# Waits on landed gathers in GpSimd's queue of a four-layer graph network

## The reference

```python
edge_index = jnp.stack([src, dst])
x = x + L0_gnn(layernorm(x), edge_index)   # attention over 4 heads of the rows x[src[:n]] and x[dst[:n]], n = 3125
x = x + L0_ffn(layernorm(x))               # the best 1561 of the nodes go through a 256-1024-256 network
x = x + L1_gnn(layernorm(x), edge_index)   # relu(segment_sum((x @ W)[src] * norm, dst) + b)
x = x + L1_ffn(layernorm(x))               # attention over 64 slices, 8 heads
x = x + L2_gnn(layernorm(x), edge_index)   # as L1_gnn, with other weights
x = x + L2_ffn(layernorm(x))               # mixture of 8 experts, the best two per node
x = x + L3_gnn(layernorm(x), edge_index)   # graph attention, 8 heads: softmax over the edges of a target
x = x + L3_ffn(layernorm(x))               # mixture of 8 experts, two for all nodes
```

## Time and profile before

| what | value |
|---|---|
| median of 3 runs | 2577.74 us |
| lowest and highest run | 2570.55 and 2579.27 us |
| profiled execution, first to last instruction (span) | 2994.7 us |
| its time around the span | not given |
| PE busy | 2247.6 us, 75% |
| VectorE busy | 1684.2 us, 56% |
| GpSimd busy | 1306.1 us, 44% |
| ScalarE busy | 561.2 us, 19% |
| bytes moved by DMA | 252.62 MB, of them 206.43 MB by gathers |

### The profile page before, as it was taken

How to read it: one execution, slowest core, us unless ns; L and a number is a source line. 1 busy time by engine, 2 the same in 40 slices (tenths; PEclk the granted TensorE clock), 3 DMA queues, 4 the chain that set the end, 5 groups by cost and what they waited for, 6 DMA issues and landing times.

```text
span 2994.7 us, 35813 instructions
## 1 busy us (share of the span) xinstructions
PE 2247.6 (75%) x10818; PEld 1674.7 (56%) x10819; DVE 1684.2 (56%) x4704; ACT 561.2 (19%) x1129; POOL 1306.1 (44%) x1347
## 2 busy tenths in 40 slices
PE   1359955576778778915888978897688888887797
PEld 1347743344444444714766767775566666665576
DVE  2585424455546564835566666656567676765343
ACT  1332310011111111301222222232011101110232
POOL 7101135566556530065555565501666666662000
PEclk8669976798888897957898988998677787777899
DMA  6100032333333313164444444401333333331100
GB/s 186 38 4 25 26 93 78 87 101 95 88 94 96 99 55 102 52 196 122 123 123 121 117 128 120 121 7 62 89 88 91 87 89 88 90 87 30 39 12 24
DMA packets 118568, 252.62 MB, mean 84 GB/s; under 512 B 35491, under 2 KB 61469, under 8 KB 118414
## 3 DMA queue, kind: packets, MB, share of 16 engines
q0 software_dynamic: 70816, 206.43, 25.0%
q1 hardware_dynamic: 44382, 44.41, 4.7%
q10 hardware_dynamic: 3216, 0.01, 0.1%
HBM read 229.33 MB, written 21.43 MB: 84 GB/s over the span
## 4 chain that ended last, share of the span: by engine, by line
PE 45%; DVE 19%; another core or an unknown queue 15%; issue 14%; ACT 3%; DVEq 3%; POOL 1%; DMA 0%; ACTq 0%; SPq 0%
PE PB L990 6%; DVE ACC L1729 6%; PE PB L863 4%; PE PB L637 3%; PE PB L588 3%; PE PB L555 3%; PE PB L640 3%; PE PB L543 2%; PE PB L874 2%; PE PB L582 2%; PE PB L954 2%; PE PB L806 2%; PE PB L969 1%; DVE ACC L2215 1%
## 5 line engine op out<-in xcount | busy, mean ns | idle before, releaser
L453 POOL DMA_INDIRECT BIG<-table,SRCI x832 | 825.1, 992 | 707.4 <-DMA table<-ACC 234.5
L1729 DVE TENSOR_TENSOR ACC<-ACC,PB 128x256 f32 x832 | 348.5, 419 | 540.2 <-remote 249.9
L453 POOL DMA_INDIRECT BIG<-parts,SRCI x416 | 399.1, 959 | 467.5 <-DMA parts<-BIG 197.3
L990 PE MATMUL PB<-BIG,WA 128*128 128x264 f32 x832 | 355.1, 528 | 72.5 <-DVE BIG L2119 46.5
L637 PE MATMUL PB<-BIG,OH 128*128 128x256 f32 x832 | 268.3, 452 | 145.5 <-DVE ACC L1729 123.2
L640 PE MATMUL PB<-BIG,OH 128*128 128x256 bf16 x1248 | 190.5, 296 | 131.6 <-DVE ACC L1729 94.7
L637 PEld LDWEIGHTS PB<-BIG,OH 128*128 128x128 f32 x832 | 164.0, 219 | 182.1 <-DVE ACC L1729 116.1
L640 PEld LDWEIGHTS PB<-BIG,OH 128*128 128x128 bf16 x1248 | 125.8, 105 | 191.1 <-issue 112.0
L2215 DVE TENSOR_TENSOR ACC<-ACC,PB 128x264 f32 x416 | 176.9, 425 | 85.0 <-PE PB L990 46.1
L2119 DVE TENSOR_TENSOR BIG<-BIG 128x256 f32<-128x256 f32 x416 | 157.1, 419 | 117.3 <-ACT BIG L1270 112.5
L863 PE MATMUL PB<-XT,WA 128*128 128x256 f32 (+1 forms) x832 | 215.2, 412 | 10.2 <-ACT HT L1232 10.2
(11 more groups left out here) (465 smaller groups left out, 3318.3 us busy)
## 6 DMA issues: line engine op xcount, KB each, us to landing
BIG<-table,SRCI POOLq DMA_INDIRECT x832
BIG<-parts,SRCI POOLq DMA_INDIRECT x416
table<-ACC SPq DMA_DIRECT2D x10, 660.0 KB, 3.4
swtab<-HT SPq DMA_DIRECT2D x25, 256.0 KB
BIG<-swtab SPq DMA_DIRECT2D x25, 256.0 KB, 3.9
parts<-BIG SPq DMA_DIRECT2D x5, 960.0 KB, 4.1
X<-in_x SPq DMA_DIRECT2D x1, 3072.0 KB
out<-X SPq DMA_DIRECT2D x4, 640.0 KB
```

What stands on the lines that cost most here:

```text
L453: g.indirect_dma_start(out=ring[:, k * width:(k + 1) * width], out_offset=None, in_=rows, in_offset=bass.IndirectOffsetOnAxis(ap=SRCI[:, n ...
L990: pe.matmul(PB[k % 4][:, 0:ROW], OH4[:, (q * GRP + k) * P:(q * GRP + k + 1) * P], G[:, (q * GRP + k) * ROW:(q * GRP + k + 1) * ROW], start ...
L1729: v.tensor_tensor(dst, dst, bank[:, k % 2 * D:(k % 2 + 1) * D], ALU.add).then_inc(sem(f"{st}_acc"), 1)
```

## The change

GpSimd gets three more kinds of wait, and nothing else changes: no gather, buffer or size, and no other engine's program. In the head attention it waits, before the ten gathers of a chunk, until the ten of the chunk ahead have landed. Before the first gather of dst it waits for the last chunk, and after each eight of them for the last four ahead. In gather_slots it waits before each group but a stage's first until the eight gathers of the group ahead have landed; that wait stands in front of the one for PE.

```diff
             for t in range(NT):
+                if t and t % CH == 0:
+                    g.wait_ge(sem(f"g0_in{t // CH - 1}"), 16 * 2 * CH)
                 for buf, n in ((FROM_COL, t), (FROM_ROW, NT + t)):
                     g.indirect_dma_start(out=buf[:, t * D:(t + 1) * D], out_offset=None, in_=a["x"],
...
             g.wait_ge(sem("d_given"), 2)
             for t in range(NT):
+                if t % 8 == 0:
+                    if t:
+                        g.wait_ge(sem(f"d_in{(t // 4 - 1) % 4}"), 16 * 4 * ((t // 4 - 1) // 4 + 1))
+                    else:
+                        g.wait_ge(sem(f"g0_in{NC - 1}"), 16 * 2 * CH)
                 if t >= D_RING and t % 4 == 0:
                     g.wait_ge(sem("d_within"), t - D_RING + 4)
...
                 for n in range(SLOTS):
                     q = n // GRP % NG
                     if n % GRP == 0:
+                        if n:
+                            g.wait_ge(sem(f"slot_in{(q - 1) % NG}"), landed_before(st) + 16 * GRP * ((n - GRP) // BODY + 1))
                         g.wait_ge(sem(f"{st}_mm"), n + GRP)
```

## The result

| | before | after |
|---|---|---|
| median of the runs (4 and 4, side by side) | 2574.14 us | 2822.64 us |
| lowest and highest | 2569.98 and 2579.27 | 2817.98 and 2830.22 |
| ratio after to before | | 1.0972, 95% interval 1.0943 to 1.1 |

The change makes the kernel slower by 248 us. The prediction said slower, by 145, and its range ended at 2810.

A forecast was written before the change was run, and what follows sets the result against it. Without holding back, GpSimd's gather issue is as near the bound as PE; with the waits GpSimd binds. Stages 1847 against 1702 us, other terms nothing: 2577.7 + 145 = 2723 us; forecast range 2640 to 2800, whole range 2480 to 2810.

The forecast's parts named there:

- The reading of the 417 us: Profiled span over run median: increments held back while gathers flow, mostly absent in timed runs; 50 us start, 367 stages.
- Step 1: Waits before 153 groups in the three gather stages: each adds a landing, GpSimd becomes the bound, 1847 against 1702, +145 us.
- Step 2: Same group waits, with the skill's fixed cost of about 2.0 us per DMA replacing the three gaps: +168 us, not adopted.
- Steps 3 and 4: Waits in head attention and among gathers of dst: covered by other work, 0 of a possible 8 and 5 us.
- A: Rival: holding back is in the timed runs too, at VectorE's adds and the start; faster, 2393 or likelier 2485; chance 0.27.
- B: Rival: gather issue in timed runs is cheaper than 1.25 us, so the wait is hidden; no change, 2578 us; chance 0.13.
- C: Rival: full price everywhere, GpSimd never waiting for PE before; 153 x 1.7 = +260, 2838 us; chance 0.06.
- the ring of four groups: Gather stages: it hides nothing of a longer period, being full once at a stage's start and drained once.
- Gaps never at 0.30: Sign in the changed kernel's profile: gaps before each group of gathers at least 1.3 to 2.1 us, never 0.30.
- the "remote" waits: Sign: VectorE's waits for late semaphores without visible cause; the longest at L1729 gone, their sum below 150 us.
- PE waiting for gathers: Sign in the changed kernel's profile: PE waits for gathers in the stages, which it did not do before.
- The span near 2810: Sign: profiled span falls from 2994.7 by 185 us to about 2810, as the waits remove holding back.

The follow-up runs named there:

- the own work: Four GpSimd memsets of 240 columns before each group, no wait for a landing, added to the kernel before: 2657.6 us, ratio 1.0363.
- the late wait: Kernel before with the wait for the group ahead placed before each group's second gather, in all three stages: 2649.8 us, ratio 1.0305.
- the one-stage kernels: Kernel before plus one stage's waits: first 2672.2 us, third 2660.9 without held increments; 2924.8, 2989.8 and 3008.0 (first, second, third) with them.

## Why the prediction was right in its sign and wrong in its size

**The reading of the 417 us** as held increments that the compared runs don't have was right, and with it the sign. The stage total that followed from it, 1702 us, was measured at 1704 to 1707 in a profile without holds; the 417 us it had split into 50 for the start and 367 for the stages are 57 (first gather at 418.7 and 362.2) and 365 between the two profiles. The group times of 10.12, 10.75 and 10.79 us lie near the issue floors of 10.0, 10.0 and 10.6, the second furthest above. The cause it gave was wrong: the prediction put the holds down to the recording, and profiled executions without any hold show that recording alone doesn't bring them.

**Step 1, the price of the added wait in the convolutions, is the step that failed**: the term of 11.58, 11.76 and 11.9 us a group was too small. Its mechanism is shown: the own work gives the bound, the late wait gives the price as elapsed time, and the one-stage kernels give the place. Its parts, in us a group:

| stage | group, predicted | measured | eight issues, predicted | measured (mean) | gap, predicted | measured (mean) |
|---|---|---|---|---|---|---|
| first | 11.58 | 12.16 | 9.70 | 9.84 | 1.88 | 2.33 |
| second | 11.76 | 12.37 | 9.70 | 9.84 | 2.06 | 2.53 |
| third | 11.9 | 12.61 | 10.29 | 10.54 | 1.6 | 2.06 |

0.58 + 0.61 + 0.71 = 1.90 us, times 52 is 99 us, against 103 missing in the runs and 111 between the two profiles (256 and 145). In the profiles most of the rest is the tail behind the last group of each stage, 28 us in the three stages where the prediction had 14 for PE's matmuls alone. Of the 1.90 us three quarters (1.38) are the gap. The prediction took it from the earlier trace rows, where GpSimd had been released by PE or by a late increment in a held stretch, and never by the landing itself; one row stood for a stage. In the changed kernel the semaphore is full 2.04, 2.27 and 1.80 us after the last gather's end on the mean (1.83, 2.14, 1.80 the median), and GpSimd starts 0.26 to 0.29 us behind that. The one row that the prediction had for the move itself (data until 1.5 us after the end) was right for the data and left out both the rest of the way to the semaphore and the waking. The other quarter is the issue: in the first two stages a mean was needed and the median of 0.946 was taken, while single gathers take 1.2 to 2 us; in the third the mean is 1.05 and not the 1.024 of the earlier trace rows.

**Step 2**, the 2.0 us of the Trainium skill ("DMA: Bandwidth & Descriptors", section "Anatomy of one DMA — SWDGE (gpsimd) path") in place of the rows, gave +168, nearer to +248 than the rows' +145, and left out the section's second term, the bytes by 436e9 a second. With it (128 rows of 1056 and of 1536 bytes: 0.31 and 0.45 us) the estimate from that page of the Trainium skill is 52 x (9.70 + 2.31 + 9.70 + 2.45 + 10.29 + 2.31) + 14 - 1702 = +224 us, and the gaps 2.31, 2.45 and 2.31 us stand beside measured medians of 2.12, 2.40 and 2.06. With rows of 256 bytes the estimate is 2.08, and 1.75 was measured: counted from the end of the gather's instruction, the constant part in these traces is smaller and the part of the bytes larger than in that section.

**Steps 3 and 4**, nothing for the head attention and for the gathers of dst: right (0.9991). Among held increments the same waits gain 52 us, where the prediction had said some 45 for the start. Its other two sums for that condition were 73 us less for the first stage (74 measured) and 45 and 20 less for the other two (9 less and 9 more).

**The rivals.** A (the holding is in the compared runs) fell for the verdict; the same mechanism decides in the other condition, where two parts of the change gain 74 and 52 us. The rule of the Trainium skill cited for it ("NOTIFIC — the notification-queue block", section "10. Constraints, capacities, measured rates": an implicit record costs an engine no time) fits the profiled executions of 2571.8 and 2572.9 us without any hold. It isn't tested by them, since every run on record has a recorded span. B (a gather's issue cheaper without recording) fell: 0.30 and 0.95 us stand in the profiles whose spans are the runs' times. C, the full price, came nearest with 2838: it charged 1.7 us for each of 153 waits, and 248 / 153 = 1.62. That is partly luck: a wait costs 2.0 us in the first stage, 1.2 in the second and 1.8 in the third (102, 62 and 90 us by 51), and no stage has C's figure. Its condition (nothing to hide in) holds in the first and third stage, where every seam was at 0.30. In the second GpSimd had waited for PE at some seams: the mean gap was 0.91 us (in the kernel with the first stage's waits only), so that 2.53 costs 1.62 a group; and of these 83 us 20 came back, since PE, which ended 33 us after the second stage's last gather had started, ended 13 us after it in the changed kernel. That is the one place where the ring of four groups hid something, against the prediction's sentence that it hides nothing. The range left it out by 13 us: with a main term read from single rows, its upper end should have taken C in.

**The profile of after.** Gaps never at 0.30, the "remote" waits gone and PE waiting for gathers came as said; but the "remote" waits are gone without the change too, so that sign tells nothing of it. The span near 2810 was right in number (2828.5) and for a reason that did not apply: the profiled execution had no holds to lose.

## What to carry to other kernels

Find the engine whose instructions follow each other without a gap over a whole stage: here GpSimd, 44% busy by the page, with 0.30 us between 1.25 us steps, which no busy share shows. A wait for one's own transfers in such a queue costs the whole landing each time (here 2.1 to 2.5 us from the last issue to the next), less what is issued between; put it two groups back, where it is free, or behind a few more gathers. And where a profile's span is far from the runs' times, settle first which one of the two the comparison will have: the same two lines of code were worth −74 us in the one and +102 in the other.

## What the runs showed of the hardware that was not expected

- Semaphore increments, PE's above all, are held back while gathers are issued without a stop, up to 13 us at VectorE's adds, in one group of runs and in none of the others (4 groups, 37 runs of before, all within 2559 to 2579 us), with the same kernel, recorded alike. The one group ran on a chip of its own. A stop of about 2 us after each eight gathers removes it in the first stage (134.7 us of such waits to 5.2) and not wholly in the second (106.7 to 47.6). The cause is open.
- From the end of a gather's instruction to the next instruction that waits for its landing: 1.75 us with rows of 256 bytes, 2.12 with 1056, 2.40 with 1536 (medians). With 1056 bytes in the third stage it is 2.06. The last 0.26 to 0.29 us of it, on the mean, lie between the semaphore's last increment and the start of the waiting instruction.
- A gather of 128 rows costs GpSimd 0.94 us and 0.30 to the next, with 256, 1056 or 1536 bytes a row.
- With waits between the groups PE's granted clock is lower (0.95 to 0.88 in the first stage), while it does the same work with longer pauses.
